# Cross-attention in another order: query groups of one block, and the first scores moved

## The reference

```python
x = x + L0_xattn(layernorm(x), ctx, ctx, ...)      # 16 heads over features, rotary
x = x + L0_ffn(layernorm(x), ...)                  # router, 2 of 16 experts, shared part
x = x + L1_xattn(layernorm(x), ctx, Wq, Wk, Wv)    # 32 heads of 8
x = x + L1_ffn(layernorm(x), ...)                  # router, low-rank experts on a base product
```

```python
q = rms(layernorm(x[b]) @ Wq.T);  k = rms(ctx[b] @ Wk.T);  v = ctx[b] @ Wv.T
x[b] += softmax(q @ k.T / sqrt(8)) @ v             # for each of 32 heads
```

## Time and profile before

| | us |
|---|---|
| median of 3 runs (377.31 to 382.29) | 377.38 |
| the profiled execution | 376.17 |
| its span, first to last instruction | 374.4 |
| PE busy | 300.2 (80%) |
| DVE busy | 263.4 (70%) |
| ACT busy | 180.3 (48%) |
| POOL busy | 109.3 (29%) |
| mean granted TensorE clock, as a share of full | 0.886 |

### The profile page before, as it was taken

The page is one execution under the profiler, slowest core; times in us unless marked ns, Lnnn a source line. Parts: engine busy times, 40 slices in busy tenths (PEclk is TensorE's granted clock), DMA queues, the critical chain, the costliest instruction groups (busy, mean ns, idle before and its releaser), DMA issues.

```text
span 374.4 us, 7224 instructions
## 1 busy us (share of the span) xinstructions
PE 300.2 (80%) x2650; PEld 193.9 (52%) x2650; DVE 263.4 (70%) x677; ACT 180.3 (48%) x301; POOL 109.3 (29%) x216
## 2 busy tenths in 40 slices
PE   4367988888896885899998899994269586896996
PEld 3223444445453442587665899973146354563464
DVE  6967879898798784666932366635886558798783
ACT  1112476675766656516442376731257557572211
POOL 1134255373453122200772011227751011210000
PEclk9755799999999999959999699997567888799899
DMA  7593458668577796100225278786742974900011
GB/s 239 166 266 113 119 165 258 182 193 266 139 246 215 213 225 242 57 1 0 83 102 172 85 216 278 253 263 182 217 124 84 264 212 119 248 8 3 0 56 56
DMA packets 77426, 59.23 MB, mean 158 GB/s; under 512 B 5072, under 2 KB 74192, under 8 KB 77392
## 3 DMA queue, kind: packets, MB, share of 16 engines
q1 hardware_dynamic: 67728, 43.73, 40.3%
q10 hardware_dynamic: 8128, 10.85, 9.2%
q0 software_dynamic: 1536, 4.20, 3.5%
HBM read 33.92 MB, written 25.69 MB: 159 GB/s over the span
## 4 chain that ended last, share of the span: by engine, by line
PE 38%; DVE 28%; DMA 9%; issue 9%; POOL 9%; ACT 4%; SPq 2%; DVEq 0%; POOLq 0%; ACTq 0%
DVE mx L1738 9%; PE psum L769 4%; PE psum L1080 4%; POOL sorted_x L1602 4%; PE psum L1092 4%; PE psum L716 3%; DVE rope_ab L1727 2%; PE psum L733 2%; PE psum L1159 2%; PE psum L929 2%; DMA qstk<-mT 2%; PE psum L754 2%; PE psum L1068 2%; PE psum L976 2%; PE psum L897 1%
## 5 line engine op out<-in xcount | busy, mean ns | idle before, releaser
L1738 DVE TENSOR_REDUCE mx<-psum 128x2 f32<-128x512 f32 x128 | 80.3, 682 | 16.0 <-PE psum L733 15.8
L1214 ACT ACTIVATE prob<-psum 128x1024 f32<-128x1024 f32 x64 | 64.0, 1023 | 31.6 <-PE psum L754 31.1
L733 PE MATMUL psum<-kstk,qstk 64*128 64x256 bf16 x256 | 38.2, 295 | 13.0 <-DMA kstk<-stack_scratch 8.9
L769 PE MATMUL psum<-prob,vt 128*32 128x256 f32 x512 | 35.0, 384 | 5.4 <-ACT prob L1214 4.2
L1447 ACT ACTIVATE prob<-psum 128x1024 f32<-128x1024 f32 x32 | 32.0, 1023 | 9.2 <-PE psum L1036 9.2
L733 PEld LDWEIGHTS psum<-kstk,qstk 64*128 64x128 bf16 x256 | 15.7, 98 | 27.3 <-DVE mx L1738 13.4
L1055 PE MATMUL psum<-prob,vt 128*32 128x128 f32 x512 | 24.4, 317 | 4.9 <-ACT prob L1447 4.9
L754 PE MATMUL psum<-qstk,kstk 64*128 64x256 bf16 x256 | 25.1, 279 | 3.4 <-DMA qstk<-mT 3.3
L769 PEld LDWEIGHTS psum<-prob,vt 128*32 128x32 f32 x512 | 16.1, 109 | 13.4 <-ACT prob L1214 5.8
L1979 DVE COPY xnT<-psum 128x512 f32<-128x512 f32 (+1 forms) x16 | 10.6, 668 | 15.5 <-PE psum L1068 15.5
L754 PEld LDWEIGHTS psum<-qstk,kstk 64*128 64x128 bf16 x256 | 8.1, 95 | 23.9 <-issue 15.3
(11 more groups left out here) (254 smaller groups left out, 611.8 us busy)
## 6 DMA issues: line engine op xcount, KB each, us to landing
qstk<-stack_scratch SPq DMA_DIRECT2D x32, 256.0 KB, 4.4
stack_scratch<-parts SPq DMA_DIRECT2D x23, 192.0 KB, 2.1
kstk<-key_scratch SPq DMA_DIRECT2D x16, 256.0 KB, 4.7
prob<-sorted_x SPq DMA_DIRECT2D x15, 256.0 KB, 4.1
kstk<-stack_scratch SPq DMA_DIRECT2D x14, 256.0 KB, 5.4
stack_scratch<-parts SPq DMA_DIRECT2D x25, 128.0 KB, 2.1
sorted_x<-zero_row ACTq DMA_DIRECT2D x3, 1024.0 KB, 5.8
wup<-in_wup ACTq DMA_DIRECT2D x4, 640.0 KB, 4.8
```

The costliest lines, as they stand in the source:

```text
L733: last = nc.tensor.matmul(misc(u + s)[:, nb * D:(nb + 1) * D], qstk[par][rows, pair, nb * P:(nb + 1) * P], kstk[par][rows, pair, :], start ...
L769: last = nc.tensor.matmul(pv_bank(1)[32 * j:32 * j + 32, g * D:(g + 1) * D], vt[b % 2][:, mb, 4 * t + j, 8:40] if low else vt[b % 2][:, mb ...
L1214: nc.scalar.activation(prob[(b * PAIRS + k) % 3][:], exp_buf(k).rearrange("p a n -> p (a n)"), ACT.Exp, scale=SCALE).then_inc(exp_done, 1)
L1738: nc.vector.tensor_reduce(mx[:, half, :, 4 * s + p4:4 * s + p4 + 1], bank.rearrange("n (b m) -> n b m", b=2), AX_X, ALU.max).then_inc(misc ...
```

## The change

Queries of blocks 2 and 3 become groups of their own; pairs 4,5 and 6,7 stay and are renumbered to groups 4 and 5. On PE, the projections of blocks 2 and 3 come ahead of the first scores, and the first scores wait for block 0's freed bank (`("qT", 0)`) and stand behind block 1's flip. SP starts the six key loads of blocks 0 to 2 when the gathers of block 3 have landed, instead of those of block 1. Block 4's experts are added by ACT and POOL instead of DVE, blocks 4 and 5 are centred on ACT instead of DVE, and the pieces of the groups have new places among the exponentials and in DVE's and POOL's lists.

```diff
...
         C_STEPS = 4
-        GROUPS = [(0,), (1,), (2, 3), (4, 5), (6, 7)]
+        GROUPS = [(0,), (1,), (2,), (3,), (4, 5), (6, 7)]
...
-        C_PRO = [(("xT", 0), 6), (("q", 0), 5), (("xT", 1), 7), (("q", 1), 4), (("qT", 0), 0),
-                 (("xT", 2), 6), (("qT", 1), 1), (("q", 2), 5)]
-        C_SLOTS = {0: {1: ("xT", 3), 5: ("qT", 2)},
-                   1: {1: ("q", 3), 4: ("o", 0)},
-                   2: {0: ("qT", 3), 4: ("o", 1), 5: ("xT", 4)},
-                   3: {1: ("q", 4), 4: ("o", 2)},
-                   4: {0: ("qT", 4), 4: ("o", 3)},
+        C_PRO = [(("xT", 0), 6), (("q", 0), 5), (("xT", 1), 7), (("q", 1), 4), (("qT", 0), 0), (("xT", 2), 6),
+                 (("q", 2), 7), (("xT", 3), 6), (("q", 3), 5), (("qT", 1), 6)]
+        C_SLOTS = {0: {4: ("qT", 2), 5: ("xT", 4)},
+                   1: {4: ("qT", 3), 6: ("q", 4), 7: ("o", 0)},
+                   2: {4: ("o", 1), 5: ("xT", 5), 6: ("qT", 4)},
+                   3: {3: ("q", 5), 4: ("o", 2)},
+                   4: {2: ("qT", 5), 4: ("o", 3)},
                    5: {2: ("dxT", 0), 3: ("dxT", 1), 4: ("o", 4), 5: ("dxT", 2), 6: ("dxT", 3), 7: ("dh", 0)},
...
         def home(use):
-            return 5 if use[0] in ("q", "dh", "dlg") or use in (("qT", 3), ("qT", 4)) or use[0] == "dxT" and use[1] % 2 else 4
+            return 5 if use[0] in ("q", "dh", "dlg") or use in (("qT", 4), ("qT", 5)) or use[0] == "dxT" and use[1] % 2 else 4
...
         C_ORDER = [use_ for use_, _ in C_USES]
-        C_FREED = [{("q", 1): ("qT", 0), ("qT", 0): ("q", 1)}.get(use_, use_) for use_ in C_ORDER]
+        SINGLE = [(kind_, g_) for g_ in range(4) for kind_ in ("q", "qT")]
+        C_FREED = SINGLE + [("o", 0), ("q", 4)] + [use_ for use_ in C_ORDER if use_ not in SINGLE + [("o", 0), ("q", 4)]]
...
             sp.wait_ge(k_fill, 16)
-            sp.wait_ge(gathered[1], 32)
+            sp.wait_ge(gathered[3], 32)
             for b in range(SETS):
                 keys_c_from_dram(b)
-            for b in range(2):
+            for b in range(4):
+                if b >= SETS:
+                    keys_c_from_dram(b)
                 queries_c_to_dram(b)
                 queries_c_from_dram(b)
-            queries_c_to_dram(2)
-            queries_c_to_dram(3)
-            queries_c_from_dram(2)
-            keys_c_from_dram(3)
-            queries_c_from_dram(3)
             for b in (4, 6):
...
                     if b < 2:
+                        wait_freed(pe, (("qT", 1), ("q", 2))[b])
                         pe.wait_ge(v_copied, b + 1)
...
             for use, _ in C_PRO:
-                if use == ("qT", 1):
-                    wait_bank(pe, ("q", 2))
-                    wait_freed(pe, ("xT", 2))
-                    project_queries(2, 0)
-                c_use(use, done=int(use == ("q", 2)))
-            wait_freed(pe, ("qT", 1))
+                c_use(use)
+            wait_freed(pe, ("qT", 0))
             scores_c(0, 0, 0)
...
                     if spot in C_SLOTS[b]:
-                        c_use(C_SLOTS[b][spot], done=int(C_SLOTS[b][spot] in (("q", 3), ("q", 4))))
-                    if b in (0, 2) and spot == 7:
-                        wait_bank(pe, ("q", 3 + b // 2))
-                        wait_freed(pe, ("xT", 3 + b // 2))
-                        project_queries(3 + b // 2, 0)
+                        c_use(C_SLOTS[b][spot], done=int(C_SLOTS[b][spot] in (("q", 4), ("q", 5))))
+                    if (b, spot) in ((1, 5), (3, 1)):
+                        g = 4 + b // 2
+                        wait_bank(pe, ("q", g))
+                        wait_freed(pe, ("xT", g))
+                        project_queries(g, 0)
...
                 if g >= 2:
-                    wait_freed(act, ("q", g - 1))
-                at = D * (g == 1)
+                    wait_freed(act, ("q", g - 2 if g < 4 else g - 1))
+                at = D * (g % 2) if g < 4 else 0
                 nc.scalar.activation(sq[:, at:at + wide], c_bank(use)[:, 0:wide], ACT.Square).then_inc(sq_done, 1)
...
             def center(b):
-                act.wait_ge(mean_ready, b - 5)
+                act.wait_ge(mean_ready, b - 3)
                 nc.scalar.activation(xn[b % 2][:], xall[:, b, :], ACT.Identity, bias=nmean[:, b:b + 1]
...
             take_x_c(2)
+            scale_experts(4)
+            squares(2)
+            take_x_c(3)
             scale_experts(5)
+            squares(3)
             first_parts_c(1)
             second_parts_c(1)
-            scale_experts(6)
-            squares(2)
-            scale_experts(7)
...
                     if k == 0:
-                        if b == 1:
-                            second_parts_c(2)
-                        if b in (2, 4):
-                            first_parts_c(2 + b // 2)
+                        if b == 3:
+                            second_parts_c(4)
+                        if b == 0:
+                            scale_experts(6)
+                        if b == 2:
+                            for x in GROUPS[5]:
+                                center(x)
                         if b == 6:
...
                         if b == 0:
-                            take_x_c(3)
-                        if b in (1, 3):
-                            squares(3 + b // 3)
-                        if b in (2, 4):
-                            second_parts_c(2 + b // 2)
+                            scale_experts(7)
+                        if b == 4:
+                            first_parts_c(5)
                     if k == 2:
+                        if b == 0:
+                            first_parts_c(2)
+                            center(4)
                         if b == 1:
-                            for x in GROUPS[4]:
-                                center(x)
+                            first_parts_c(3)
+                        if b == 3:
+                            squares(5)
+                        if b == 4:
+                            second_parts_c(5)
                         if b == 5:
...
                     if k == 3:
+                        if b in (0, 1):
+                            second_parts_c(2 + b)
                         if b == 0:
-                            first_parts_c(2)
-                        if b == 2:
+                            center(5)
                             take_x_c(4)
+                        if b == 1:
+                            squares(4)
+                        if b == 2:
+                            take_x_c(5)
+                            first_parts_c(4)
                         if b == 5:
...
                 else:
-                    wait_freed(pool, ("xT", 4))
+                    wait_freed(pool, ("xT", 5))
                 nc.gpsimd.tensor_scalar(xn[n % 2][:], xall[:, n, :], nmean[:, n:n + 1], rstd[:, n:n + 1],
...
             def add_experts(b):
-                pool.wait_ge(scaled, b - 4)
+                pool.wait_ge(scaled, b - 3)
                 steps.then(nc.gpsimd.tensor_tensor(gather_buf(b, 0), gather_buf(b, 0), gather_buf(b, 1), ALU.add))
...
+            add_experts(4)
             add_experts(5)
...
             add_experts(6)
-            add_experts(7)
             third_c(2)
+            add_experts(7)
             fill_values(2)
-            fill_values(3)
             third_c(3)
+            fill_values(3)
+            third_c(4)
             fill_values(4)
             fill_values(5)
-            third_c(4)
+            third_c(5)
             fill_values(6)
...
                     pass
-                elif first < 5:
+                elif first < 4:
                     add_experts(first, n)
                 else:
-                    dve.wait_ge(experts_added, first - 4)
+                    dve.wait_ge(experts_added, first - 3)
                 steps.then(bn_stats_of(first, n))
...
                 steps.then(last)
-                if first > 5:
+                if first > 3:
                     nc.vector.tensor_scalar(nmean[:, first:first + 1], mv[:, first:first + 1, 0], -1.0, None, ALU.mult
...
                 use, blocks = ("q", g), GROUPS[g]
-                n, at = 32 * len(blocks), D * (g == 1)
+                n, at = 32 * len(blocks), D * (g % 2) if g < 4 else 0
                 wait_filled(dve, use)
...
             root_queries(1)
-            attend_norm(4, 1)
-            dve.wait_ge(x_copied, 3)
-            center(4, 0)
             rest_queries(1)
-            attend_norm(5, 1)
-            center(5, 1)
             root_queries(2)
+            attend_norm(4, 1)
+            rest_queries(2)
+            attend_norm(5, 1)
+            root_queries(3)
...
-            attend_norm(6, 1)
-            rest_queries(2)
-            attend_norm(7, 1)
             divide_c(0)
-            root_queries(3)
-            add_attended(0)
             rest_queries(3)
+            attend_norm(6, 1)
+            add_attended(0)
+            root_queries(4)
+            attend_norm(7, 1)
```

(35 more changed lines are left out.)

2 lines of the change are left out of this document (1 added, 1 removed).

## The result

The changed kernel took 381.96 us (median of 4 runs, 378.07 to 383.29) against 377.35 for the kernel before on the same chip (4 runs, 375.69 to 382.29): ratio 1.0129, 95% interval 1.0083 to 1.0176. Later, in 12 runs beside 16 of before, it took 380.58 against 377.05: ratio 1.0057, interval 1.0014 to 1.0101. (The ratios leave disturbed runs out, the medians do not; for runs 5 to 8 only three of the eleven runs of the kernel before are left, 370.0 to 373.6 us, so their ratios say little.) So it is 3.5 to 4.6 us slower by the medians, clear of the noise but under the 2% that the prediction calls no change; forecast were 2.6. The profiled execution took 383.29 us, with a span of 381.5 against 374.4. It was the slowest of its four, and the profiled execution of the kernel before (376.17) lay 1.2 under its median, so the two traces differ by more than the medians.

A forecast was written before the change was run, and what follows sets the result against it. Hand-overs between in-order engines bound the phase, no engine alone. Block 2's scores 3.7 us earlier, then block 3 1.7 late, block 4 5.0 late, block 6 2.6 late: 377.38 + 2.6 = 380.0 us, range 373.6 to 384.0.

The forecast's parts named there:

- The new wait: In block 2, ACT's centring of block 7 waits for DVE's mean behind a pair's root; block 3's first exponential 1.7 us late.
- rival 1: Block 2's lead is kept: block 7 centred in time, the earlier stack's 3.7 us run to the end, 373.7 us (15%).
- Pair 4,5 late: Block 4's first scores wait for a query stack written later; block 4's first exponential comes 5.0 us late.
- Block 2 alone: Block 2's queries go singly, not as a pair: its first scores 3.7 us earlier, its first exponential 2.1 us ahead.
- What block 4 gives back: In block 4 the old wait for pair 6,7's root goes; block 6's first scores are only 2.6 us late.
- Rival 2: It cancels: pair 4,5 is written 2 us earlier than forecast and block 4 gives all back, 377.4 us (25%).
- E(0,0) 2.0 us earlier: Block 0's first exponential on ACT moves from 278.01 to 276.0, two weightings of experts now standing behind it.
- Rival 3: Key loads push back block 0's query stack: first scores at 277.6, all 2.0 us later, 382.0 us (17%).

The follow-up runs named there:

- run 5: Changed kernel with DVE's attend_norm(7) and root_queries(4) ahead of add_attended(0), pair 4,5 projected at block 1's step 5: 379.92 us against 377.04, ratio 1.0116.
- run 6: Changed kernel with DVE's attend_norm(7) ahead of add_attended(0) and divide_c(1) ahead of root_queries(4): 380.03 us against 377.04, no ratio.
- run 7: As run 6, with the key loads behind gather 1 instead of gather 3: 378.86 us against 377.04, ratio 1.0151.
- run 8: Changed kernel with key stacks 1 and 2 loaded behind query stacks 0 and 1: 380.48 us against 377.04, ratio 1.0258.
- run 12: Changed kernel once more, unedited: 380.58 us against 377.05 for the kernel before, ratio 1.0057.
- run 1: Changed kernel with DVE's attend_norm(7) ahead of add_attended(0) and root_queries(4): 380.38 us against 377.09, ratio 1.0089.
- run 9: Changed kernel with pair 4,5 projected five steps earlier, attend_norm(7) ahead of its root, divide_c(1) behind: 378.64 us against 377.29, ratio 1.0047.
- run 4: Changed kernel with the first scores waiting for block 1's qk_rest again, as before the change: 380.61 us against 377.09, ratio 1.0061.
- run 2: Changed kernel with the key loads behind gather 1 again, as before the change: 379.84 us against 377.09, ratio 1.0043.
- run 3: Kernel before with only the key loads moved behind gather 3: 380.24 us against 377.09, ratio 0.9969.
- run 11: Kernel before with only key stack 0 ahead of query stack 0, its own gate kept: 377.16 us against 377.29, ratio 1.0032.
- run 10: The edits of run 8 and run 9 together in the changed kernel: 377.19 us against 377.29, ratio 1.0009.

## Why the prediction was right, and where it was off

The time (380.0) lies within the runs' spread and its range held; the sign and the mechanism were right, the size too small. That the 380.0 lies within 2 us of both medians (380.58 and 381.96) is in part luck: counted from the first gather to the end, the trace of the changed kernel has 6.1 us more than before (run 12's 6.5) where 2.6 were forecast, and 1.9 of the difference is a gain in the prologue that did not show. Step by step:

- **The new wait**: forecast E(2,0) to E(2,1) 6.8 us, measured 6.8; E(2,1) to E(3,0) 7.2, measured 7.0. Run 1 shows the cause of the wait, by removing it, and not its price. What the step did not see is that the root also held divide_c(1) and add_attended(1): hence run 1 gained 1.5 us of the 4.94 in that stretch and next to nothing by the end, and rival 1, that block 2's lead can be kept if block 7 is centred in time, was wrong for a reason the prediction did not give.
- **Pair 4,5 late**: forecast 9.4 us from E(3,0) to E(4,0), measured 9.7, with S(4,0) waiting 3.00 us. Shown by run 9, where the stack came in time and 7.0 remained.
- **Block 2 alone**: the two edits inside block 0 cost as forecast in sum (17.4 us to E(2,0), 16.9 forecast, 17.0 before), with blocks 0 and 1 shared differently: E(0,0) to E(1,0) took 8.7 and not 9.5, E(1,0) to E(2,0) 8.6 and not 7.4.
- **What block 4 gives back**: forecast 2.3 us less from E(4,0) to the end, measured 1.2 in this trace, 0.1 in run 12, 1.9 in run 4 and 2.6 in run 2. In run 12, S(6,0) waited 2.78 us for its stack, in the changed kernel's first trace 0.43. Rival 2 had hoped for more; it got less.
- **The term that was mis-sized: E(0,0) 2.0 us earlier.** It came 0.1 earlier. The key loads went out when forecast (262.78, less the 1.0: 261.7), and the write of block 0 moved by 0.4 us (18.2 after the first gather, 18.6 before; forecast 0.3). But the flip of block 1 on PE was late, because DVE, ACT and PE paused. DVE's timeline of the changed kernel:

```profile
270.11 0.18 DVE L2020 BATCH_NORM_AGGREGATE mv<-stats 128x2 f32<-128x6 f32 x1 [1.23 <-DVE stats L1710]
270.82 0.15 DVE L2025 TENSOR_SCALAR eps_v<-mv 128x1 f32<-128x1 f32 x1 [0.53 <-DVE mv L2020]
272.22 0.35 DVE L2030 TENSOR_SCALAR xn<-xall,mv 128x256 f32<-128x256 f32 x1 [1.24 <-DVE eps_v L2025]
```

Of the two profiles compared, only that of the changed kernel had this pause. Like with like: without such gaps between 17 and 23 us after the first gather, E(0,0) stood at 27.9 us (the kernel before) and at 26.8 and 26.2 (runs 5 and 6, the changed order and gate); with gaps of 3.0 us and more in sum at 30.5 and 30.6 (runs 3 and 11, the order of before) against 27.6 to 28.4 (the changed kernel, runs 1, 4, 9 and 12). The forecast gain of 2.0 is 1.1 to 1.7 in the first comparison and 2.1 to 3.0 in the second. It was there, and a pause covered it in that trace. The changed order is not what brings the pause, since runs 3 and 11 have it. But it does not look like chance from one execution to the next either: all eight traces of the first and the third chip have it, none of the four of the second, which are runs 5 to 8. The chip of the first two profiles is not on record, and no trace has the order of before on the second chip.

Of the span's 7.1 us, 1.0 lies ahead of the first gather, −0.1 is the prologue, and 6.2 follow E(0,0), where 4.6 were forecast. This last part does not depend on the pause. From E(0,0) to the end the order of before took 95.3 to 96.4 us (3 traces), the changed order with the wait for block 7's mean 100.9 to 103.2 (the changed kernel, runs 2, 4, 8 and 12), run 1 102.5, runs 5 to 7 98.6 to 98.8, and runs 9 and 10 99.4 and 99.9. So relieving the root won back some 2 to 4 us of it in the traces; what holds the last 2 to 3 was not found.

**Rival 3** was half right. S(0,0) at 277.64 is past the 277 that the prediction set as its limit; on the prediction's own axis, with the 1.0 us of the later first gather taken off, it is 276.6, inside the limit and 1.0 later than forecast, but not by that rival's mechanism. The loads do delay the read: SP reads 3.7 to 3.8 us behind the write where at most two loads or an early gate precede it (before and runs 2, 7, 8, 10 and 11), 4.2 to 6.0 where six stand behind gather 3 (the changed kernel and runs 1, 3, 4, 5, 6, 9 and 12). The Trainium skill (DMA: Bandwidth & Descriptors, "Queues, rings and completion order") says that each DMA engine consumes the descriptors of a ring in order. By that a short transfer starts behind what its ring holds in front; these eight traces agree, with 0.4 to 2.3 us. Yet the stack was last at S(0,0) only where there was no pause: it waited 1.24 and 1.14 us for it in runs 5 and 6, 0.56 in run 8, and in the changed kernel itself not at all. By runs 5 and 6 against run 8, which has two loads in front in place of six, the price at E(0,0) without the pause is 0.9 to 1.5 us, not 2; whether the loads cost anything in a trace with the pause is not shown (28.1 in run 9 with six in front, 28.2 in run 10 with two).

## What to carry to other kernels

When one long step is moved ahead on an in-order engine, list all that queues behind it, in order, with each one's consumer: removing the first wait uncovers the next, and here three stood behind one root. Here the split brought S(2,0) 1.3 us earlier, counted from the first gather, and made S(4,0) wait 3.0 us, because the next pair was projected later; with that projection five steps earlier the wait was gone (run 9). Compare two traces from a common event near the change and in stretches, and trust a stretch's difference only if a second profile repeats it.

## What the hardware showed unasked

- In 9 of 14 traces DVE shows gaps over 0.3 us, 2.0 to 4.3 us in sum, between an instruction and the next one, 17 to 23 us after the first gather, and ACT and PE are mostly idle beside them; in the stretch shown POOL works on. The load on the DMA engines alone does not do it. Run 10 in its pause, then run 6 at the corresponding place; columns: stretch and its length, busy us and count of PE, PEld, DVE, ACT and POOL, granted clock, DMA share, GB/s.

```profile
268.44:270.44 2.00, 0.41 (x1) 0.00 (x0) 0.39 (x2) 0.00 (x0) 1.62 (x2) 0.50 0.76 214
```

```profile
271.61:273.61 2.00, 1.45 (x4) 1.18 (x4) 1.82 (x6) 1.33 (x4) 1.67 (x3) 0.50 1.13 308
```

DVE did 0.39 us of work at a DMA share of 0.76 and 1.82 us at 1.13. The nine traces have something else in common: in the 23 us behind the first gather the profile names no releaser (issue) for 8 to 11 of the 15 to 18 waits of PE and ACT over 0.3 us, in the other five for none. ACT's copy of block 0's flip, in run 11 and in the kernel before:

```profile
256.23 0.37 ACT L1398 COPY xT<-psum 128x256 f32<-128x256 f32 x1 [4.87 <-issue]
```

```profile
257.07 0.37 ACT L1396 COPY xT<-psum 128x256 f32<-128x256 f32 x1 [4.65 <-PE psum L976]
```

So the pause comes together with events that the profile lacks, and that the profiling itself brings it is an untested rival: no run shows that unprofiled executions have it. What pauses the engines stays open.
- Single runs of one program differ more than the change is worth: the kernel before took 370.0 to 383.2 us over all its runs here, so that ratios from 6 runs have intervals up to 4% wide, and only the stretches of the traces told the steps apart.
